# Loading 97 rows of edge indices as 96 rows and one

## What is computed

```python
for l in range(2):
    xn = layernorm(x, ln1_g[l], ln1_b[l])
    deg = segment_sum(ones, src)                    # standardised over the nodes
    xp = xn + xn @ Wpos[l] + bpos[l] + deg[:, None] * Wdeg[l][0] + bdeg[l]
    q, k, v = xp @ Wq[l] + bq[l], xp @ Wk[l] + bk[l], xp @ Wv[l] + bv[l]
    att = clip(einsum('ehd,ehd->eh', q[dst], k[src]) / 4, -50, 50)
    alpha = segment_softmax(att, dst)
    x = x + segment_sum(v[src] * alpha, dst) @ Wo[l] + bo[l]
    x = x + gelu(layernorm(x, ln2_g[l], ln2_b[l]) @ W1[l] + b1[l]) @ W2[l] + b2[l]
return layernorm(x_input + x)
```

## Time and profile before

| | |
|---|---|
| median of 3 runs | 2145.94 us (2145.27 to 2147.04) |
| the profiled execution's own time | 2146.24 us |
| its span, first to last instruction | 2144.0 us |
| mean granted TensorE clock | 0.834 |
| busy: PE, DVE, ACT, POOL | 1429.2, 1457.1, 920.0, 1489.5 us |
| first gather of layer 0 starts | 115.12 us |
| HBM traffic | 149 GB/s over the span |

### The profile page before, as it was taken

The page is one execution under the profiler, slowest core; times in us unless marked ns, Lnnn a source line. Parts: engine busy times, 40 slices in busy tenths (PEclk is TensorE's granted clock), DMA queues, the critical chain, the costliest instruction groups (busy, mean ns, idle before and its releaser), DMA issues.

```text
span 2144.0 us, 44177 instructions
## 1 busy us (share of the span) xinstructions
PE 1429.2 (67%) x11694; PEld 1269.1 (59%) x11695; DVE 1457.1 (68%) x2503; ACT 920.0 (43%) x1639; POOL 1489.5 (69%) x1584
## 2 busy tenths in 40 slices
PE   2757656766777777776554666676677677777555
PEld 2547655655666666665543665565566566666554
DVE  4987766656777677676557666666677767777654
ACT  1334433334555555554225333332455555555323
POOL 0067777777777777777736777777777777777773
PEclk9868897788999889788677888777889988888767
DMA  2145555455555555555524554554455555555541
GB/s 63 39 160 174 164 164 154 155 162 155 160 171 161 159 166 165 158 165 169 160 59 158 159 160 154 160 158 153 155 163 163 161 162 158 159 166 157 168 150 52
DMA packets 120419, 321.60 MB, mean 150 GB/s; under 512 B 31428, under 2 KB 43834, under 8 KB 120320
## 3 DMA queue, kind: packets, MB, share of 16 engines
q0 software_dynamic: 75072, 205.10, 31.8%
q1 hardware_dynamic: 44410, 113.69, 16.1%
q10 hardware_dynamic: 838, 1.60, 0.3%
HBM read 311.92 MB, written 8.35 MB: 149 GB/s over the span
## 4 chain that ended last, share of the span: by engine, by line
POOL 64%; issue 22%; DVE 5%; PE 4%; DMA 1%; SPq 1%; DVEq 1%; ACT 1%; ACTq 0%; POOLq 0%
POOL kv L560 64%; DVE q_parts L837 1%; PE ps L1342 1%; DMA kv<-kv_tab,src_idx 1%; SPq L440 1%; DMA kv<-in_dst 1%; DVE msg L1104 1%; DVE qkv L924 0%; DVE dots L1080 0%; PE ps L1304 0%; SPq L441 0%; PE ps L1298 0%; PE ps L1195 0%; DVEq L356 0%; DVE prod L1070 0%
## 5 line engine op out<-in xcount | busy, mean ns | idle before, releaser
L560 POOL DMA_INDIRECT kv<-kv_tab,src_idx x1564 | 1485.7, 950 | 622.6 <-issue 474.6
L1342 PE MATMUL ps<-msg,hot 128*128 128x136 f32 x3896 | 665.3, 338 | 370.7 <-DVE acc L985 363.6
L1342 PEld LDWEIGHTS ps<-msg,hot 128*128 128x128 f32 x3896 | 613.1, 239 | 414.3 <-DVE msg L1104 237.8
L1327 PE MATMUL ps<-q_parts,hotT 128*128 x5844 | 467.5, 242 | 221.4 <-DVE prod L1070 171.3
L1327 PEld LDWEIGHTS ps<-q_parts,hotT 128*128 x5844 | 415.7, 109 | 286.0 <-issue 265.4
L1070 DVE TENSOR_TENSOR prod<-kv,ps 128x1024 f32<-128x1024 f32 (+1 forms) x198 | 238.4, 1204 | 267.6 <-DMA kv<-kv_tab,src_idx 244.1
L990 DVE SCALAR_TENSOR_TENSOR hot<-dst_col,neg_base,ps 128x1024 f32<-128x1024 f32 (+1 forms) x246 | 311.8, 1267 | 125.0 <-issue 117.2
L696 ACT ACTIVATE dist<-dst_rows,neg_node 128x1024 bf16<-128x1024 int32 x246 | 282.5, 1148 | 140.9 <-issue 126.3
L705 ACT ACTIVATE msg<-att 128x64 f32<-128x64 f32 (+1 forms) x198 | 49.9, 252 | 595.6 <-DVE att L1085 594.9
L699 ACT ACTIVATE hotT<-dist 128x1024 bf16 x246 | 259.9, 1057 | 50.1 <-ACT dist L696 44.4
L1080 DVE TENSOR_REDUCE dots<-prod 128x64 f32<-128x1024 f32 (+1 forms) x198 | 238.8, 1206 | 28.9 <-DVE prod L1070 23.9
(11 more groups left out here) (221 smaller groups left out, 972.6 us busy)
## 6 DMA issues: line engine op xcount, KB each, us to landing
dst_rows<-in_dst SPq DMA_DIRECT2D x194, 512.0 KB, 4.1
kv<-kv_tab,src_idx POOLq DMA_INDIRECT x1564
kv_tab<-qkv SPq DMA_DIRECT2D x26, 128.0 KB
kv_tab<-qkv SPq DMA_DIRECT2D x3, 768.0 KB, 3.8
out<-z SPq DMA_DIRECT2D x24, 64.0 KB
hot<-in_L_gnn_W SPq DMA_DIRECT2D x2, 256.0 KB
w<-in_L_gnn_W SPq DMA_DIRECT2D x2, 256.0 KB
kv_tab<-qkv SPq DMA_DIRECT2D x1, 512.0 KB, 3.8
```

What stands on the lines that cost most here:

```text
L560: pool.indirect_dma_start(kv[:, u, c, :], None, kv_tab[l][:, :], bass.IndirectOffsetOnAxis(ap=src_idx[:, c, at(g)], axis=0)).then_inc(kv_i ...
L1327: last = MM(qd[:, c * P:(c + 1) * P], hotT[:, bass.ds(pr % 2, 1), c * P:(c + 1) * P], q_parts[:, at(t), k * D:(k + 1) * D], start=first an ...
L1342: last = MM(agg, hot[:, u % 2, c, :], msg[:, u % 2, c, :], start=(c == 0), stop=(c == nch - 1))
```

## The change

The load of rows 2 to 98 of each buffer becomes a load of rows 3 to 98 (96 rows) in the same place, and a load of row 2 alone, which stands in the second loop ahead of those of rows 1 and 0, behind the wait for DVE's fills. That makes eight edge loads instead of six; ACT waits for 128 instead of 96. Nothing is computed otherwise, and every byte lands where it did.

```diff
             for rows, d in ((src_i, src_d), (dst_i, dst_d)):
-                sp.dma_start(rows[2:NG, :], d[FIRST + SECOND:E].rearrange("(g e) -> g e", e=GE)).then_inc(edges_in, 16)
+                sp.dma_start(rows[3:NG, :], d[FIRST + SECOND + GE:E].rearrange("(g e) -> g e", e=GE)).then_inc(edges_in, 16)
             sp.wait_ge(rows_clear, 2)
             for rows, d in ((src_i, src_d), (dst_i, dst_d)):
+                sp.dma_start(rows[2:3, :], d[FIRST + SECOND:FIRST + SECOND + GE].rearrange("(g e) -> g e", g=1)).then_inc(edges_in, 16)
                 sp.dma_start(rows[1:2, 0:SECOND], d[FIRST:FIRST + SECOND].rearrange("(g e) -> g e", g=1)).then_inc(edges_in, 16)
...
-            act.wait_ge(edges_in, 96)
+            act.wait_ge(edges_in, 128)
```

## The result

The changed kernel took 2115.87 us, the median of 4 runs (2113.33 to 2117.99), beside 2145.99 for the kernel before, of 4 runs too (2145.27 to 2147.04). The ratio is 0.986, with a 95% interval of 0.9847 to 0.9872. That is 30.1 us less; 28.5 were forecast. The profiled execution took 2117.99 us, 28.3 less than that of before, for a span of 2115.7. From the added line, 440, on, the lines of the kernel have numbers higher by one.

What follows compares the result with a forecast made beforehand. POOL's gather pace fixes the time from the first gather on, so the edge-load wait before it counts fully. 28.8 less 0.3, with zero for the clock, gives 28.5 us: 2117.4 us, own range 2115.9 to 2118.4, wider 2113.5 to 2122.

Steps and rivals of the forecast that it cites:

- The bound: Before the first gather at 115 us: one DMA engine carries both 97-row loads; time there counts one for one.
- 96 rows on all engines: Edge loads: 96 rows use sixteen engines, ending ACT's wait near 11.5 us instead of 42.83; one-engine rival, chance 0.05.
- The first term: PE's transposes begin behind its fourth block at 16.08 us instead of 44.89, 28.8 us earlier; block seven at 26.4.
- The second term, `x`: DVE's statistics: `x` lands at 15.3 to 17.4 us, 16 taken, free up to 16.4; late-`x` rival, chance 0.06.
- The third term, the clock: TensorE's clock in transposes and folding: taken as zero, ends -4.0 and +6 us; slower-TensorE rival, chance 0.09.
- that rival: TensorE faster in transposes (1.7 us) and folding (2.3 us): gain 32.5 us, 2113.5 us; chance 0.07.
- The 0.3 us taken off for a late ACT or `x`: Ahead of block seven: 0.3 us subtracted from the 28.8 for ACT or `x` slightly late, leaving 28.5.

Runs made afterwards that it cites:

- E3: The changed kernel with both edge loads split as 89 rows and 8 instead of 96 and 1: ratio 1.0004 to the kernel before.
- E2: The changed kernel with only the source rows split into 96 and 1, the destination rows one load of 97: ratio 0.9973 to the kernel before.
- E7: The changed kernel a third time, no edit: 2116.66 us beside 2145.85 for the kernel before, ratio 0.9861.
- E11: E6 a second time, the changed kernel with only the transposes one count block earlier on PE: 2117.42 us, ratio 0.9867.
- E4: The changed kernel with both edge loads split as 95 rows and 2 instead of 96 and 1: ratio 0.9915 to the kernel before.
- E6: The changed kernel with the 32 transposes one count block earlier on PE: 3245.97 us beside 3278.17 for the kernel before, ratio 0.9903.
- E8: The changed kernel with the transposes one count block earlier and the last 53 rows of `x` loaded as 48 and 5: 2116.89 us, ratio 0.9866.
- E10: The changed kernel with the 53 rows of `x` issued ahead of its 24 tiles and the transposes one count block earlier: 2115.57 us, ratio 0.9862.
- E5: The kernel before with only the last 53 rows of `x` loaded as 48 and 5, edge loads left at 97 rows: ratio 0.9993.
- E1: The changed kernel again, no edit: 3198.13 us beside 3228.72 for the kernel before, ratio 0.9912.
- E9: The changed kernel with ACT's two loads of `x` in the other order, 53 rows ahead of the 24 tiles: 2116.53 us, ratio 0.9868.

## Why the prediction was right

**The bound.** That one of sixteen DMA engines carried both loads, and that the time ahead of the first gather counts one for one, held. E3 shows that the number of rows decides, not the split, and E2 that each load of 97 rows had its own share. POOL's wait fell by 28.3 us and the profiled execution by 28.3. In all seven profiled executions at this pace (before, changed, E7 to E11), on three chips, the whole time less the start of the first gather is 2030.5 to 2031.2 us, with first gathers from 83.76 to 115.12.

**96 rows on all engines.** This was taken from the divisibility of 97, 53 and 128 rows. The trace after confirms it: 0.93 of all engines busy at 262 GB/s up to 10 us, and the edges in at 10.8; 11.5 was forecast. E4's five packets at a time for 95 rows fit the rule of the Trainium skill, "DMA: Bandwidth & Descriptors", section "Why a DMA increments its semaphore by 16 and not by 1", by which 95 rows run on five.

**The first term.** Transposes forecast at 16.1, found at 15.88; what ends last is PE's block and not a load, as forecast. ACT was in time. Its second issue did not shorten to nothing: it was held for 6.55 us, and ended at 9.13 instead of 13.07, early enough. In E7 it ended at 10.04, and ACT's line began only at 11.44, straight behind its table load, without moving block seven.

**The second term, `x`.** Forecast at 15.3 to 17.4 with 16 taken; found at 15.2 to 15.9 in the three runs of the changed kernel, so it cost nothing. The point from which it would was put at 16.4; by the block seven found it is 26.19 - 10.0 = 16.2. The 10.0 us from the statistics to block seven hold in all five runs in which `x` came last (E4, E6, E8, E10, E11). E8 and E11, with `x` at 16.4 and 16.5, are beyond the point: block seven at 26.37 and 26.49, later than 26.19 in spite of earlier transposes. Block seven was forecast at 26.4 and began at 26.19, 29.0 us earlier than before.

**The third term, the clock.** Taken as zero with ends of -4.0 and +6. The transposes took 7.11 us (7.15 before), so PE's denser work changed nothing there. That they could fall to 3.8 was misread: they stood at the higher level already. The kernel before:

```profile
44.90:52.00 7.10, 7.10 (x35) 7.08 (x36) 0.00 (x0) 1.80 (x2) 0.00 (x0) 1.00 0.01 2
```

So the 1.7 us of that rival could not come, and its price was at most the 2.3 of the folding. In the folding DVE's wait for PE was 3.0 us instead of 2.3, which takes 0.7 of the 29.0: 28.3. The clock itself did change: the kernel before has the lower level twice in the folding (0.52 from 58 to 60 us, and again from about 69), the changed one only from about 40 us on, which is the second of the two. The higher clock between 28 and 40 us gave nothing, since DVE has no wait for PE there. The stretch from 42 to 44 us, changed kernel:

```profile
42.00:44.00 2.00, 1.90 (x20) 1.79 (x20) 0.65 (x2) 1.44 (x5) 0.00 (x0) 0.50 0.45 126
```

Over all runs that wait was 1.2 us (E5, E10) to 3.3 (E2): the same 28 blocks and folding differ by up to 2.1 us in this place. The waits lie around the time at which the granted clock falls to 0.50, and that time varies, but no run isolates it: the cause is not shown.

**The size.** 28.5 forecast, 28.3 by the profiled executions, 30.1 and 29.2 by medians on two chips. The 0.3 us taken off for a late ACT or `x` was not lost; 0.7 was, in the folding, where the sum had nothing. That the two nearly cancel, with a first term 0.2 larger, is luck. The median of 2115.87 lies a hair under the forecast's own range of 2115.9 to 2118.4. Behind the two median gains stand single runs near 2113.4 beside others near 2117 for the same changed kernel, and of before 2142.0 beside 2146.8; the 1.8 us by which the first median gain exceeds that of the traces are in that scatter. Its cause is not settled.

**Left open** is why all kernels took 3200 us on two chips. There, POOL waited for DVE; in E1 the profile puts PE's idle time ahead of line 1328 down to "issue" (367 us beside 18 in the changed kernel's first trace) and 474 us of DVE's ahead of line 1071 to "remote", which was nothing there, and names no cause.

## What to carry to other kernels

Before reading any load as slow because it is large, look at the DMA share of the stretch: 0.07 is near one engine of sixteen, at 25 GB/s where a full stretch has 245 and more, and the fix is the number of rows, not of bytes. A wait of another engine that lies inside a longer one (`x`, 15.5 us) is worth nothing until the longer one is gone, and is then the next to look at: price how late it may come, here up to 16.2 us, where it came at 15.2 to 15.9. That left so little that two later edits of the transposes' place gained nothing (E8, E11). A load off the critical path can still hold it, by sharing its one engine (E5) or, if it stands behind it, its queue (E9).

## What the runs showed of the hardware

- A DMA engine that works alone moved 25 GB/s (before, 10 to 30 us); with nearly all sixteen busy they moved 262, some 18 for each busy engine (changed kernel, 2 to 10 us), and in E4 a busy engine moved 16 up to 10 us and 20 from 14 to 16 us. So the rate of a lone engine is too high for one of several.
- Of the packets of whole rows, at most one was under way at a time for 97 rows (before, from 10 us on), five for 95 (E4) and sixteen for 96 (changed kernel).
- A small load issued behind one of 24 tiles was held on its queue for 6.5 to 8.0 us (changed kernel, E1, E6 to E8, E11). Issued ahead of it, both issues took 1.4 us (E9).
- With the last 53 rows of `x` loaded as 48 and 5, the loads of 97 edge rows, which had shared their engine with them, let ACT begin 1.25 us sooner (E5).
- The kernel before took 2145 to 2146 us on three chips and 3229 and 3278 on two others, at a mean granted clock of 0.83 to 0.85 on the former and 0.69 to 0.70 on the latter (but for one execution at 0.57, which took 3246 us), while the changed kernel's first gather came at 86.26 and 86.79 us on two of the former and at 86.64 on one of the latter.
